# Mixture-of-experts rows that carry token, gate and residual, and a scatter of finished rows instead of gathers

## Chip, cores and metric

The kernel runs as one program on one core of a Trainium2 chip. The metric is the device time of one execution in microseconds (us), smaller is better.

## What is computed

The input is 2048 tokens (4 batches of 512) of 128 features, in fp32. Six residual steps follow each other: FFN, causal attention of two kinds, FFN, mixture of experts (MoE), linear attention, MoE. The change touches the two MoE steps and what feeds and follows them:

```python
def _L1_ffn_ref(x, Wr, W1, W2):                 # x: layernormed tokens, 8 experts, capacity 256
    probs = softmax(xf @ Wr); eidx = argmax(probs); p_tok = probs[eidx]
    rank = number of earlier tokens with the same expert
    keep = rank < cap                           # later tokens of a full expert are dropped
    xe = xf[dispatch]                           # the rows of each expert
    h = maximum(einsum('ecd,edf->ecf', xe, W1), 0)
    ye = einsum('ecf,efd->ecd', h, W2) * (p_tok * valid)
    y = zeros.at[dispatch].add(ye)              # back to the tokens; a dropped token gets 0

x = x + 0.5 * _L1_ffn_ref(_layernorm(x), ...)   # MoE 0
x = x + _L1_attn_ref(_layernorm(x), ...)
x = x + 0.5 * _L1_ffn_ref(_layernorm(x), ...)   # MoE 1, the result
```

## The kernel before

The five engines run programs of their own, written out by hand, which meet in semaphores. `s[...]` are semaphores, `hold` is a wait that also counts. B = 4 batches, NT = 4 tiles of 128 tokens in a batch, E = 8 experts with CAP = 256 rows, NG = 2 tiles of them. `x[b]` holds the residual stream of a batch on chip, one token to a partition and tile. Index n = 8m + e counts the experts of both MoE steps m.

The way of a token through MoE step m is this.

- `choose` and `place` on VectorE (DVE) pick the expert, the gate (`gate_all`, line 1034) and the slot of every token (`slot_all`, line 1040). A dropped token gets a spare slot behind the 2048 real ones.
- `scatter` on GpSimd (POOL, line 569) sends the layernormed rows (128 floats) of a batch to their slots in the DRAM array `xe_scr`, by four indirect DMAs of 128 rows each. In the first MoE step they lie between the `rsqrt` steps of the layernorms, in the second in the loop at line 698.
- `experts` on SyncE (SP, the queue of plain DMAs, line 479) loads an expert's 256 rows (`rows_in`) into one of four buffers `xg`, and stores the finished rows (`answer`) in slot order to `ye_scr`.
- TensorE (PE, line 1670) turns the rows, multiplies by the two weights; ScalarE (ACT) and DVE apply the relu, and DVE copies the product out of PSUM (line 1218). The order is the same in every expert: `up(e+1)`, `turn_rows(e+2)`, `down(e)`.
- After all eight experts, `gather` on POOL (line 577) fetches a batch's finished rows back from `ye_scr` by `slot_all`, again by four indirect DMAs, and `combine` on DVE (line 1220) multiplies by the gate and adds to `x[b]`. After MoE 1 sixteen indirect DMAs (line 720), sixteen DVE steps (line 1371) and four stores of `x[b]` to `out` (line 538) end the program.

The spare part of `xe_scr` is never read; the real part is set to zero in the first microseconds (line 344), since an expert with fewer than 256 tokens leaves slots empty. The stores at lines 339 to 347 and these share the semaphore `pad_zero`, which SP (line 424), DVE (line 1191) and `scatter` wait for.

The linear attention begins per batch with `combine`, `moments` (DVE), `rsqrt` (POOL), `normalise_entry` (DVE) and `turn_entry` (PE). Batches 0 and 1 are entered one after the other, batches 2 and 3 inside the loop over `attend`. The batch ends with `leave`, `normalise_exit`, `choose`, `place_exit` and the next `scatter`.

## Time and profile before

| | us |
|---|---|
| runs shown | 706.55, 710.32, 709.92 (median 709.92) |
| the profiled execution's own time | 705.89 |
| its span (first to last instruction) | 704.1 |
| PE busy, matmul | 506.5 (72%) |
| PE busy, weight loads | 323.5 (46%) |
| DVE busy | 365.7 (52%) |
| ACT busy | 196.7 (28%) |
| POOL busy | 181.9 (26%) |
| DMA, bytes moved | 74.16 MB, 105 GB/s on average |

The span is cut into stages by the semaphores. In us from its start: first FFN to 108, attention to 355, second FFN and placing to 415, experts of MoE 0 to 453, fetching rows and entering the linear attention to 500, the linear attention to 632, last scatter and experts of MoE 1 to 676, the end to 704. An engine's busy share over the whole span is a mean over these stages, and a change counts only where the chain of waits passes. The chain of waits lists, in order of time, the work that ended last; DMA there is a transfer that was waited for, "issue" is time in which the engine waited for nothing that the profile shows. The granted clock of PE is 1.0 or 0.5 of 2.4 GHz in a stretch, a value between them is a mean.

### The profile page before, as it was taken

The numbers are of one execution on the slowest core, as the hardware profiler recorded it, in microseconds if no ns is written. First come the engines' busy times: TensorE is split into PE (matmuls) and PEld (weight loads), VectorE is DVE, ScalarE is ACT, GpSimd is POOL, SyncE is SP. The second block draws the span as 40 slices with busy tenths as digits, with TensorE's granted clock in tenths as the row PEclk, the third lists the DMA queues.
The fourth block names the chain that finished last, engine by engine and source line by source line (L and its number), as shares of the span: only waits on it lengthen the run. The fifth ranks groups of instructions, "written<-read, shape, count | busy, mean of one in ns | idle before, by whom it ended". The sixth has DMA issues, their size and how long they took to land.

```text
span 704.1 us, 9924 instructions
## 1 busy us (share of the span) xinstructions
PE 506.5 (72%) x3706; PEld 323.5 (46%) x3706; DVE 365.7 (52%) x950; ACT 196.7 (28%) x278; POOL 181.9 (26%) x208
## 2 busy tenths in 40 slices
PE   1777775998899999988686639634788888735930
PEld 1654322445444544533475528522454655424920
DVE  4555482668667676820655412135778777330221
ACT  1454313451543245065235002112123111101200
POOL 8564360000101010010023350044402022031035
PEclk9999896999999999999999559956999999656975
DMA  7537877332633422060430021107652620001213
GB/s 267 210 117 244 266 246 197 120 99 62 139 101 89 126 80 80 29 159 15 134 106 16 19 64 49 38 27 178 186 149 54 190 70 16 1 16 52 61 41 101
DMA packets 61471, 74.16 MB, mean 105 GB/s; under 512 B 6772, under 2 KB 38128, under 8 KB 61168
## 3 DMA queue, kind: packets, MB, share of 16 engines
q1 hardware_dynamic: 59376, 69.34, 33.6%
q0 software_dynamic: 2048, 4.20, 2.1%
q8 instruction: 29, 0.48, 0.3%
q14 instruction: 18, 0.15, 0.1%
HBM read 42.97 MB, written 30.41 MB: 104 GB/s over the span
## 4 chain that ended last, share of the span: by engine, by line
PE 46%; DVE 17%; POOL 8%; SPq 8%; issue 8%; DMA 7%; ACT 5%; POOLq 0%; DVEq 0%; ACTq 0%
PE ps_accum L1379 21%; PE ps_pair L1379 15%; PE ps_turn L1379 5%; POOL xe_scr L574 3%; DMA sb_ring<-sb_qs 3%; SPq L358 2%; DVE sb_work L1133 2%; PE ps_turn L1387 2%; POOL sb_work L720 2%; POOL sb_rstd L558 2%; DVE sb_work L1271 2%; DVE sb_mpart L1059 1%; SPq L352 1%; DVE sb_stats L960 1%; DVE sb_values L969 1%
## 5 line engine op out<-in xcount | busy, mean ns | idle before, releaser
L812 ACT ACTIVATE sb_work<-ps_pair 128x1024 f32<-128x1024 f32 x80 | 80.3, 1026 | 50.7 <-PE ps_pair L1379 49.8
L1379 PE MATMUL ps_pair<-sb_ring,sb_xsets 128*128 128x512 f32 x160 | 64.6, 480 | 11.4 <-DMA sb_ring<-sb_qs 5.7
L1059 DVE TENSOR_REDUCE sb_mpart<-ps_turn 128x4 f32<-128x512 f32 x80 | 55.0, 687 | 31.2 <-PE ps_turn L1379 31.1
L1059 DVE TENSOR_REDUCE sb_mpart<-ps_accum 128x4 f32<-128x512 f32 x80 | 55.0, 688 | 19.2 <-PE ps_accum L1379 18.2
L1379 PE MATMUL ps_accum<-sb_work,sb_v_aug 128*32 128x128 f32 (+3 forms) x768 | 57.7, 394 | 0.3 <-ACT sb_work L812 0.3
L1379 PE MATMUL ps_turn<-sb_ring,sb_m_sets 128*128 128x512 f32 x80 | 39.5, 494 | 10.0 <-DVE sb_mpart L1059 9.8
L1379 PE MATMUL ps_accum<-sb_ring,sb_m_sets 128*128 128x512 f32 x80 | 41.8, 523 | 4.5 <-DVE sb_mpart L1059 3.9
L1379 PEld LDWEIGHTS ps_pair<-sb_ring,sb_xsets 128*128 128x128 f32 x160 | 30.7, 199 | 22.5 <-issue 10.7
L624 POOL TENSOR_TENSOR sb_e_pad<-sb_v_next,sb_y_ar 128x128 f32<-128x128 f32 x16 | 7.3, 457 | 127.2 <-DVE sb_y_ar L1103 127.2
L1271 DVE TENSOR_TENSOR sb_work<-ps_pair,sb_cst 128x1024 f32<-128x1024 f32 x32 | 37.5, 1214 | 2.2 <-PE ps_pair L1379 2.2
L1133 DVE TENSOR_TENSOR sb_work<-ps_pair,sb_cst 128x1024 f32<-128x1024 f32 x32 | 37.7, 1218 | 0.9
L556 POOL TENSOR_SCALAR sb_ve<-sb_mv 128x4 f32<-128x4 f32 x24 | 5.6, 233 | 124.5 <-DVE sb_mv L963 124.3
L1379 PE MATMUL ps_pair<-sb_y_tmp,sb_mw 128*128 128x256 f32 x128 | 34.1, 414 | 1.9 <-ACT sb_y_tmp L862 1.9
L574 POOL DMA_INDIRECT xe_scr<-sb_values,sb_slot_all x16 | 15.9, 994 | 73.4 <-DVE sb_slot_all L1040 69.8
L1387 PE MATMUL ps_turn<-sb_cst,sb_values 128*128 128x128 f32 x48 | 10.3, 354 | 34.1 <-DVE sb_values L969 29.6
L1379 PE MATMUL ps_accum<-sb_mw,sb_work 128*128 128x128 f32 x256 | 31.3, 276 | 2.3 <-issue 2.3
L1379 PE MATMUL ps_pair<-sb_xs,sb_w1r 128*128 128x512 f32 x64 | 22.1, 470 | 15.0 <-DVE sb_xs L979 7.4
L1379 PEld LDWEIGHTS ps_accum<-sb_mw,sb_work 128*128 128x128 f32 x256 | 30.0, 192 | 2.8 <-issue 2.6
L1218 DVE COPY sb_e_pad<-ps_accum 128x256 f32<-128x256 f32 x16 | 6.8, 425 | 44.7 <-PE ps_accum L1379 44.7
L1379 PE MATMUL ps_pair<-sb_ring,sb_ka_stk 128*128 128x512 f32 x64 | 24.4, 492 | 7.6 <-DVE sb_work L1271 4.9
L734 ACT COPY sb_xnT<-ps_turn 128x512 f32<-128x512 f32 x16 | 9.3, 583 | 70.6 <-PE ps_turn L1387 70.6
L1379 PEld LDWEIGHTS ps_pair<-sb_y_tmp,sb_mw 128*128 128x128 f32 x128 | 25.4, 210 | 6.6 <-ACT sb_y_tmp L862 3.4
(242 smaller groups left out, 1002.2 us busy)
## 6 DMA issues: line engine op xcount, KB each, us to landing
sb_m_sets<-q_scr SPq DMA_DIRECT2D x16, 256.0 KB
sb_xsets<-k_scr SPq DMA_DIRECT2D x16, 256.0 KB
sb_ka_stk<-mk_scr SPq DMA_DIRECT2D x4, 1024.0 KB
sb_mw<-in_mw SPq DMA_DIRECT2D x16, 256.0 KB, 5.6
sb_ka_stk<-mk_scr SPq DMA_DIRECT2D x8, 512.0 KB
q_scr<-sb_qs SPq DMA_DIRECT2D x12, 256.0 KB, 3.1
k_scr<-sb_ks SPq DMA_DIRECT2D x12, 256.0 KB, 3.9
sb_ring<-k_scr SPq DMA_DIRECT2D x64, 48.0 KB
```

What stands on the lines that cost most here:

```text
L358: sp.dma_start(ring[VW * hl:VW * hl + 3 * HD, i, hl].bitcast(F32), head_rows(q_scr, b, HL * hs + hl, 3 * HD)).then_inc(done, 16)
L558: pool.tensor_tensor(rstd[i][:], ve[i][:], const("minus_half"), ALU.pow).then_inc(s["rstd"], 1)
L574: pool.indirect_dma_start(xe_scr, bass.IndirectOffsetOnAxis(ap=places[:, t:t + 1], axis=0), rows_out[:, t, :], None).then_inc(s["scattered ...
L624: pool.tensor_tensor(dst, value, answer, ALU.subtract).then_inc(s["err_pad"], 1)
L720: pool.indirect_dma_start(y_last[:, b, t, :], None, ye_scr, bass.IndirectOffsetOnAxis(ap=slot_all[:, i:i + 1], axis=0)).then_inc(last_gath ...
L734: act.copy(dst, bank[:]).then_inc(s["x2_ready"], 1)
L812: act.activation(banks[:, 2 * i:2 * i + 2], pair[u % 2][:], ACT.Exp, scale=SCALE).then_inc(s["exp_done"], 1)
L1059: dve.tensor_reduce(mpart[:, m // NPAIR, m % NPAIR, :], max_banks[m % 2][:].rearrange("p (h k) -> p h k", h=HL), AX.X, ALU.max).then_inc(s ...
L1133: dve.tensor_tensor(work[:, n % 4].rearrange("p a (h q) -> p (a h) q", h=HL), pair[n % 2][:].rearrange("p a (h q) -> p (a h) q", h=HL), bc ...
L1271: dve.tensor_tensor(work[:, n % 4].rearrange("p a (h q) -> p (a h) q", h=HL), pair[n % 2][:].rearrange("p a (h q) -> p (a h) q", h=HL), bc ...
L1379: return pe.matmul(dst, lhsT, rhs, start=start, stop=stop, skip_group_check=True)
L1387: last = pe.transpose(tile(dst, t), src[:, t, :], ident)
```

## The change

Each expert row becomes RW = 258 floats wide: the layernormed row (128), the token number (`ID`), the gate (`GATE`), and the residual row (`OLD`, 128). There is an `xe_scr` and a `y_scr` for each MoE step. DVE writes residual, gate and token number straight into the row buffers (`wide_rows`, which lies over the attention's `ring`, for MoE 0; the two buffers of `exit_rows` for MoE 1). The residual is also stored by token to `y_scr` (`keep_old`), which serves dropped tokens. The copy out of PSUM becomes two DVE steps, product times gate plus residual. POOL converts an expert's token numbers to integers and scatters the finished rows to `y_scr` while the next expert computes. After MoE 0, SP loads `x[b]` from `y_scr`; after MoE 1 one DMA copies `y_scr` to `out`. The 1 MB of `xe_scr` rows and the spare half of `ye_scr` are no longer zeroed at the start. In their place six DMAs per program fill both `xe_scr` with harmless rows just ahead of the loads of the expert weights: four of 2048 pieces of 512 B, two of 2048 pieces of 8 B. `ring` is set to zero again by POOL before `scatter_back(0)`.

```diff
+RW = 2 * D + 2
+ID, GATE, OLD = D, D + 1, D + 2
+        "spill_ids": np.kron(NTOK + (NTOK // P) * p + np.arange(NTOK // P)[None, :], [[1.0, 0.0]]),
 # SP, at the start: four zeroing DMAs of 512 KB removed; pad_zero is waited for as 80, was 144
-            for half in range(2):
-                r0 = half * NTOK // 2
-                for dst in (xe_scr[r0:r0 + NTOK // 2], ye_scr[NTOK + r0:NTOK + r0 + NTOK // 2]):
-                    sp.dma_start(dst.rearrange("(p r) d -> p r d", p=P), zero[:, 0:1024]).then_inc(s["pad_zero"], 16)
 # SP, after the attention's last loads, ahead of the expert weights
+            for scr in xe_scr:
+                spill = scr[0:NTOK].rearrange("(p r) d -> p r d", p=P)
+                for c, src in ((0, bc(const("ident"), NTOK // P)), (OLD, bc(const("ident"), NTOK // P)),
+                               (ID, const("spill_ids").rearrange("p (r d) -> p r d", d=2))):
+                    sp.dma_start(spill[:, :, c:c + src.shape[2]], src).then_inc(s["spill_in"], 16)
+            def keep_old(m, b):
+                sp.dma_start(tile_rows(y_scr[m], b), rows_out[m][b][:, :, OLD:RW]).then_inc(old_kept[m][b % 2], 16)
             def experts(m):
-                sp.wait_ge(s["scattered"], 16 * NT * B * (m + 1))
+                for i in range(2):
+                    sp.wait_ge(sent[m][i], 16 * NT * B // (m + 1))
+                    hold(sp, old_kept[m][i], 16 * B // (m + 1))
+                sp.wait_ge(s["spill_in"], 96)
                 for e in range(4):
                     rows_in(m, e)
-                for e in range(E):
-                    if e + 4 < E:
-                        rows_in(m, e + 4)
-                    answer(m, e)
+                for e in range(4, E):
+                    rows_in(m, e)
+                for kept in ye_kept:
+                    hold(sp, kept, 16 * E * (m + 1))
             def rows_in(m, e):
                 if n >= 4:
                     sp.wait_ge(s["xg_t"], n - 3)
+                    sp.wait_ge(s["places_in"], n - 3)
+                    sp.wait_ge(s["ye_evac"], n - 3)
+            for b in range(B):
+                hold(sp, s["ffn_x"], B + b + 1)
+                keep_old(0, b)
             experts(0)
+            for b in range(B):
+                sp.dma_start(x[b][:], tile_rows(y_scr[0], b)).then_inc(x_loaded[b], 16)
+            hold(sp, s["zeroed"], 18)
 # SP, loop of the linear attention: keep_old(1, b - 1) after load_l1(b + 1, 1)
             experts(1)
-            for b in range(B):
-                sp.wait_ge(s["mixed"], NT * (B + b + 1))
-                sp.dma_start(tile_rows(out, b), x[b][:]).then_inc(s["out_done"], 16)
+            sp.dma_start(out.rearrange("(p r) d -> p (r d)", p=P),
+                         y_scr[1][0:NTOK].rearrange("(p r) d -> p (r d)", p=P)).then_inc(s["out_done"], 16)
 # POOL
+            def places_of(n):
+                pool.wait_ge(xg_loaded[n % 4], 16 * (n // 4 + 1))
+                if n >= 4:
+                    pool.wait_ge(ye_kept[n % 2], 16 * NG * ((n - 2) // 2))
+                pool.tensor_copy(places_back[:, n % 4, :], xg[:, n % 4, :, ID]).then_inc(s["places_in"], 1)
+            def scatter_back(m):
+                for kept in old_kept[m]:
+                    hold(pool, kept, 16 * B // (m + 1))
+                places_of(E * m)
+                for e in range(E):
+                    n = E * m + e
+                    if e + 1 < E:
+                        places_of(n + 1)
+                    pool.wait_ge(s["places_in"], n + 1)
+                    hold(pool, s["ye_evac"], n + 1)
+                    for g in range(NG):
+                        pool.indirect_dma_start(y_scr[m], bass.IndirectOffsetOnAxis(ap=places_back[:, n % 4, g:g + 1], axis=0),
+                                                ye[n % 2][:, g, :], None).then_inc(ye_kept[n % 2], 16)
 # POOL: scatter(m, b) of rows_out[m][b] into xe_scr[m]; its first call of a step also waits for spill_in 96
+            pool.memset(ring[:, 0:2].bitcast(F32), 0.0).then_inc(s["zeroed"], 1)
+            pool.memset(ring[:, 2, 0, 0:B * NT * RW - 2 * HL * T].bitcast(F32), 0.0).then_inc(s["zeroed"], 1)
+            scatter_back(0)
-            gather(0)                       # and gather(1) to gather(3) among the rsqrt, base and low_queries
...
-            for b in range(B):              # line 717: the sixteen gathers
-                for t in range(NT):
...
+            scatter_back(1)
 # DVE, place
-                dve.scalar_tensor_tensor(out=gate_all[:, NT * b:NT * (b + 1)],
+                dve.scalar_tensor_tensor(out=rows_out[r // B][b][:, :, GATE],
                                          in0=r1[6][:], scalar=0.5, in1=r1[3][:],
                                          op0=ALU.mult, op1=ALU.mult)
+                dve.tensor_scalar(rows_out[r // B][b][:, :, ID], spare[:], float(-NTOK), None, ALU.add)
 # DVE, experts
-                    dve.tensor_copy(ye[:, n % 2].rearrange("p g d -> p (g d)"), accum[n % 2][:, 0:NG * D]).then_inc(s["ye_evac"], 1)
+                    for g in range(NG):
+                        last = dve.scalar_tensor_tensor(out=ye[n % 2][:, g, :], in0=accum[n % 2][:, g * D:(g + 1) * D],
+                                                        scalar=xg[:, n % 4, g, GATE:GATE + 1], in1=xg[:, n % 4, g, OLD:RW],
+                                                        op0=ALU.mult, op1=ALU.add)
+                    last.then_inc(s["ye_evac"], 1)
 # DVE: combine(b) becomes entry(b): wait for x[b]'s load, then moments; the sixteen steps at line 1371 go
```

The order of POOL moves at two places. Around the experts of MoE 0, from the last scatter to the second `rsqrt`, it read before (`L585` is a gather, `sb_h_act` and `sb_v_low` are buffers of the linear attention):

```order
L676 MEMSET sb_v_high 128x1024
L679 MEMSET sb_h_act 128x32 x2
L679 MEMSET sb_v_low 128x32
L679 MEMSET sb_v_high 128x32
L585 DMA sb_e_pad<-ye_scr,sb_slot_all 128x128 x4
L556 TENSOR_SCALAR sb_ve_0<-sb_mv_0 128x4
L558 TENSOR_TENSOR sb_rstd_0<-sb_ve_0,sb_cst 128x4
L585 DMA sb_e_pad<-ye_scr,sb_slot_all 128x128 x4
```

and of the change (`sb_places_back` are the integer token numbers, `sb_y_tmp0` and `sb_y_tmp1` hold finished rows; line numbers are those of the changed file):

```order
L703 MEMSET sb_v_high 128x32
L706 MEMSET sb_ring 128x4096
L707 MEMSET sb_ring 128x32
L596 CAST sb_places_back<-sb_expert_rows 128x2 x2
L610 DMA y_scr0<-sb_y_tmp0,sb_places_back 4096x128 x2
L596 CAST sb_places_back<-sb_expert_rows 128x2
L610 DMA y_scr0<-sb_y_tmp1,sb_places_back 4096x128 x2
```

The pair of the last two rows repeats with the buffers in turn, to eight scatters of two DMAs, and the first `rsqrt` follows directly; no gather is left.

On SP the end of the program read before (`L494` loads an expert's rows, `L500` stores them):

```order
L494 DMA sb_e_pad<-xe_scr 128x2x128 x5
L500 DMA ye_scr<-sb_e_pad 128x2x128
L494 DMA sb_e_pad<-xe_scr 128x2x128
L500 DMA ye_scr<-sb_e_pad 128x2x128 x5
L538 DMA out<-sb_x 128x4x128 x4
```

and of the change, from the last `keep_old`:

```order
L483 DMA y_scr<-sb_exit_rows 128x4x128 x3
L504 DMA sb_expert_rows<-xe_scr 128x2x258 x8
L551 DMA out<-y_scr 16x16384
```

The eight stores of finished rows have left SP for POOL, and four stores of `x` have become one copy from DRAM to DRAM, laid out as 16 pieces of 64 KB.

## Rows read from the trace of the kernel before

**Rows 1.** Page, chain that ended last: shares of the span by engine.

```profile
PE 46%; DVE 17%; POOL 8%; SPq 8%; issue 8%; DMA 7%; ACT 5%; POOLq 0%; DVEq 0%; ACTq 0%
```

**Rows 2.** Timeline after the last experts: start us, us, engine line op, tiles, count, idle before.

```profile
675.82 0.42 DVE L1218 COPY sb_e_pad<-ps_accum 128x256 f32<-128x256 f32 x1 [2.16 <-PE ps_accum L1379]
678.83 1.00 POOL L720 DMA_INDIRECT sb_work<-ye_scr,sb_slot_all  x1 [41.15 <-DMA ye_scr<-sb_e_pad]
...
686.38 15.26 SPq L538 DMA_DIRECT2D out<-sb_x  x4
...
697.62 0.94 POOL L720 DMA_INDIRECT sb_work<-ye_scr,sb_slot_all  x1 [0.30 <-issue]
```

**Rows 3.** Windows, the stretch of the end: busy us of each engine, PE clock, DMA share, GB/s.

```profile
677.00:704.00 27.00, 0.00 (x0) 0.00 (x0) 4.56 (x16) 0.00 (x0) 15.16 (x16) 0.54 0.29 83
```

**Rows 4.** Timeline from the last expert of MoE 0 to the first batch's entry.

```profile
452.60 0.42 DVE L1218 COPY sb_e_pad<-ps_accum 128x256 f32<-128x256 f32 x1 [2.16 <-PE ps_accum L1379]
455.64 1.02 POOL L585 DMA_INDIRECT sb_e_pad<-ye_scr,sb_slot_all  x1 [37.95 <-DMA ye_scr<-sb_e_pad]
...
462.00 1.14 DVE L1224 SCALAR_TENSOR_TENSOR sb_x<-sb_e_pad,sb_gate_all,sb_x 128x128 f32<-128x128 f32 x4 [8.98 <-DMA sb_e_pad<-ye_scr,sb_slot_all]
```

**Rows 5.** Chain of waits, transfers around the experts and two later combines: start, us, what.

```profile
412.56 2.22 DMA xe_scr<-sb_v_next,sb_slot_all
414.80 2.23 DMA sb_e_pad<-xe_scr
...
478.55 1.06 DVE sb_x L1224 x4
...
526.71 1.06 DVE sb_x L1224 x4
```

**Rows 6.** Chain of waits, the first two DMAs of a scatter in the linear attention.

```profile
587.32 0.75 issue
588.07 1.09 POOL xe_scr L574
589.15 0.31 issue
589.46 0.97 POOL xe_scr L574
```

**Rows 7.** Timeline, pace of the experts of MoE 0.

```profile
427.23 0.43 DVE L1218 COPY sb_e_pad<-ps_accum 128x256 f32<-128x256 f32 x1 [4.31 <-PE ps_accum L1379]
...
430.96 0.42 DVE L1218 COPY sb_e_pad<-ps_accum 128x256 f32<-128x256 f32 x1 [2.71 <-PE ps_accum L1379]
...
432.49 0.38 PE L1677 MATMUL ps_turn<-sb_cst,sb_e_pad 128*128 128x128 f32 x2
```

**Rows 8.** Timeline of SP around the place of the fill.

```profile
316.17 0.60 SPq L400 DMA_DIRECT2D sb_ring<-sb_qs  x1
343.01 0.35 SPq L477 DMA_DIRECT2D sb_mw<-in_mw  x1
```

**Rows 9.** Chain of waits, the first scatter of MoE 0.

```profile
378.15 1.25 POOL xe_scr L574
```

**Rows 10.** Page, DMA issues: KB of each, median us from issue to landing.

```profile
q_scr<-sb_e_pad SPq DMA_DIRECT2D x1, 1024.0 KB, 7.3
...
v_scr<-sb_values SPq DMA_DIRECT2D x4, 256.0 KB, 2.7
```

**Rows 11.** Timeline, POOL's memset of the ring, and DVE at the wait for `pad_zero`.

```profile
2.97 6.92 POOL L551 MEMSET sb_ring<- 128x8192 f32 x1
...
26.78 1.12 DVE L969 TENSOR_SCALAR sb_y_ar<-sb_x,sb_mv,sb_rstd 128x128 f32<-128x128 f32 x4 [1.58 <-POOL sb_rstd L558]
28.00 0.87 DVE L960 BATCH_NORM_STATS2 sb_stats<-sb_x 128x6 f32<-128x128 f32 x4
```

**Rows 12.** Timeline, small steps of `place`.

```profile
388.59 0.16 DVE L1033 TENSOR_TENSOR sb_r<-sb_r,sb_spare 128x4 f32<-128x4 f32 x1
388.67 0.15 DVE L1034 SCALAR_TENSOR_TENSOR sb_gate_all<-sb_r,sb_r 128x4 f32<-128x4 f32 x1
```

155 lines of the change are left out of this document (67 added, 88 removed).

## The prediction

> **What bounds the kernel now.** I read the share of the chain first: PE holds 46% of it, but DVE, POOL, the queues, transfers and "issue" hold the rest [rows 1]. So much of the time is hand-over, not arithmetic, and the two MoE steps are full of it. I then read the timeline from the end backwards. The last product leaves PSUM at 675.82 + 0.42 = 676.24. From there to the end of the span at 704.1 pass 27.9 us in which PE does nothing; POOL is busy for 15.2 us of the last 27.0 [rows 2, 3]. It issues sixteen gathers one after the other, from 678.83 to 697.62 + 0.94 = 698.56, that is 1.25 us for each; DVE's steps and the four stores of SP hang on them. The bound of the end is POOL's issue of indirect DMAs.
>
> Then I read the same place after MoE 0. The product is ready at 453.02, the first gather starts at 455.64, and the first batch's combine runs from 462.00 to 463.14 [rows 4]. Each later combine costs the chain another 1.06 us: three such pieces stand in it, the first at 478.55, the last at 526.71 [rows 5]. Between these places, the experts run at a pace that PE sets: two copies out of PSUM follow each other after 430.96 - 427.23 = 3.73 us [rows 7]. In the linear attention POOL's scatters stand on the chain too, 0.75 us of issue and then 1.09, 0.31, 0.97 us for the first two DMAs [rows 6].
>
> **The change part by part.**
>
> *The end.* Sixteen gathers, sixteen DVE steps and four stores go. In their place stands only what cannot lie beside the experts: the last expert's two scatters and the copy. The copy out of PSUM becomes two DVE steps of 128 columns. The gather's combine has four such steps in 1.14 us [rows 4], 0.29 each, so the pair costs 0.57 where 0.42 stood, +0.15: ready at 676.39. POOL then needs 0.75 of issue, 1.09 for the first DMA and 0.31 to the second [rows 6]: 678.54. A scatter lands 2.22 us after its start [rows 5]: 680.76. The copy of 1 MB I cannot read anywhere. A store of 256 KB lands in 2.7 us, one of 1024 KB in 7.3, with other stores in the queue [rows 10]. The lower bound is 2.7. The upper is 14.6, twice 7.3, if the bytes read from DRAM and the bytes written to it add. I take 6.5, near the row of equal size but with an empty queue. The end is then 687.3 instead of 704.1: **-16.8 us**, with -20.6 and -8.7 as ends. For the copy the Trainium skill, page "DMA: Bandwidth & Descriptors", section "Anatomy of one DMA — SWDGE (gpsimd) path", gives a fixed 2.0 us plus bytes at 436 GB/s; my estimate by that is 4.4 us, and the sum would be 2.1 us lower. The page's fit is of another issuing engine, and no run here shows a copy from DRAM to DRAM.
>
> *Entering the linear attention.* The same steps after 453.02: +0.15, 0.75 + 1.09 + 0.31, 2.22 to land, which is 457.54. SP then loads `x[0]`, 256 KB; a load of 128 KB takes 2.23 [rows 5], a store of 256 KB 2.7 [rows 10]; I take 3.0, so 460.5, against 463.14 before: **-2.6 us**, between -3.4 and -1.4 for loads of 2.2 to 4.2. What is late next is the same as before, `moments` on DVE.
>
> *Later combines.* Their three pieces vanish, and `moments` waits for loads that came in about 460: **-3.2 us** (3 x 1.06). DVE is in program order here and the pieces are on the chain, so I count all; the lower bound is 0, if PE or a load ends the wait in their place. The gathers among POOL's small steps go too; no wait of the chain ends on them, so 0.
>
> *The experts.* Rows grow from 512 to 1032 B. The first load of a step is on the path: 2.23 for 128 KB [rows 5]; with twice the bytes I take 2.9, and 0.1 more for the last scatter before it: +0.8 twice, **+1.6 us**, ends 0 and +4.4 (double both). In the steady state loads have slack: the load of expert 4 now waits for the first product, 427.23 + 0.6, and lands 2.9 later at 430.7, before PE wants it at 432.49 [rows 7]. POOL's work beside the experts is 0.75 + 1.09 + 0.31 + 0.97 = 3.1 us for an expert and about 0.2 for the conversion, under the 3.73 of the pace; hidden, with 0.4 to spare. The eight stores that leave SP were hidden before and save nothing.
>
> *`place`.* One step of 128x4 more, eight times. Two such steps start 388.67 - 388.59 = 0.08 us apart where none waits for the other [rows 12]; +0.08 x 8 = **+0.6 us**, from 0 to 1.3 (0.16 each).
>
> *The 32 scatters to the experts.* POOL makes as many rows as before, and 0.97 us a DMA [rows 6] was the same for 128 rows wherever I looked. I take **0**. The trace has no indirect DMA with wider rows; the upper bound is time in proportion to bytes, below.
>
> *Start.* Four zeroing DMAs go. DVE's wait for `pad_zero` ends at 28.00, and its own work before ended at 27.90 [rows 11]: 0.1 us at most, counted 0. Removing 2 MB of traffic hardly helps, since DVE and PE are not waiting for it.
>
> *The fill.* Six DMAs, 4 MB in pieces of 512 B and 4096 pieces of 8 B, go into SP's queue between 316.8 and 343.0, where SP issues nothing [rows 8]. They must be done when POOL starts the first scatter at 378.15 [rows 9]. Four times 7.3 [rows 10] is 29 us; the small pieces, priced as the 512 B ones, another 15. From about 320 that ends at 364: hidden, **0**. The expert weights behind them have until 414.80. The memset of `ring` takes about 3.5 us, half of 6.92 [rows 11], on POOL between 417 and 427, when it has nothing else; `keep_old` on SP has no one behind it who waits. Both 0.
>
> Sum: -16.8 - 2.6 - 3.2 + 1.6 + 0.6 = **-20.4 us**. Against the profiled execution's own time, 705.89, this is 685.5; the span would be 683.7. The median of the runs shown is 4 us higher, 709.92, and the four times fall into two pairs about 706 and 710. I put the forecast on their mean, 708.2: **687.8 us**.
>
> **The rivals.**
>
> *Wider rows cost POOL in proportion (slower).* If an indirect DMA with rows of 1032 B takes twice 0.97 us, each scatter adds 0.97. Of the 32, the chain passes 24: eight in MoE 0, sixteen in the linear attention, where the `rsqrt` of the next batch is queued behind them. That is +23.3 us: 711. It outweighs the gain from 0.85 us more per DMA. For it: nothing in the trace excludes it. Against: the gap between DMAs and the 0.97 look like a cost of rows, not of bytes, since gathers and scatters take the same (0.94 and 0.97). Chance 5%.
>
> *The fill is late.* If it starts only at 343 and takes 44 us, it ends at 387 and the first scatter, with `rsqrt` and the second FFN behind it, waits 9 us: 697. Should the small pieces cost several times a 512 B piece, it is more. A rule speaks for this one: the Trainium skill, page "DMA: Bandwidth & Descriptors", section "Specifications", has writes under 512 B done as read-modify-write. No small strided stores are priced in this trace. Chance 10%.
>
> *POOL does not keep the pace.* If the conversion, its wait on its own result and the two DMAs take 4.2 us instead of 3.3, POOL falls behind by 0.5 us an expert and 3.5 us by the eighth, in both steps, and DVE's reuse of `ye` waits in the end: +7, 695. For it: only 0.4 us to spare. Against: the 0.75 of issue shrinks when POOL is never idle. Chance 14%.
>
> *The copy at the end is slow.* At 14.6 us: +8.1, 696. Only 16 pieces of 64 KB, one for each DMA engine, read and written in the same memory. Chance 11%.
>
> The forecast as it stands has 60%, between 683 and 692. Slower than before needs the first rival, or two others at their worst: 6% with "over 0.5%", the least that a measurement of this kernel can tell from no change (3.5 us); within 0.5% 2%; faster 92%. The range runs from 681, where the short copy, the short loads and the lower pair of times meet, to 699, which takes in the three mild rivals.
>
> **What would show it.** In the profile after: 64 indirect DMAs on POOL, all about 0.97 us, with the `rsqrt` of each later batch directly behind; if those into `xe_scr` are longer, the first rival. PE's pace in the experts stays at 3.73, and the last scatter starts 0.75 us after the last DVE step; a larger lag is the third. From that step to the end of the span 11 us. No `L1224` pieces in the chain. The first scatter of MoE 0 still at 378, released by DVE and not by a DMA. I am wrong if the span stays above 697.

## The result, and the profile after

The changed kernel takes **685.94 us** (median of four runs, 684.23 to 691.97) beside 708.23 for the kernel before in the same comparison: a ratio of 0.970, 95% interval 0.963 to 0.977. Five more rounds gave 686.97 against 709.29, ratio 0.968 (0.963 to 0.972). The forecast was 687.8 in a range of 681 to 699, faster with 92%.

The profiled execution took 686.1 us with a span of 684.3. Its page: the chain that ended last, the costliest groups and two lines of the DMA issues (KB each, us to landing).

```profile
PE 49%; DVE 17%; POOL 8%; issue 8%; ACT 6%; DMA 5%; SPq 5%; POOLq 0%; DVEq 0%; ACTq 0%
...
L610 POOL DMA_INDIRECT y_scr<-sb_y_tmp,sb_places_back x32 | 30.8, 961 | 40.9 <-issue 33.0
...
L588 POOL DMA_INDIRECT xe_scr<-sb_exit_rows,sb_slot_all x16 | 15.9, 995 | 73.8 <-DVE sb_slot_all L1061 70.1
...
sb_expert_rows<-xe_scr SPq DMA_DIRECT2D x16, 258.0 KB, 2.8
...
xe_scr<-sb_cst SPq DMA_DIRECT2D x4, 1024.0 KB, 13.6
```

PE's share of the chain rose from 46 to 49% [rows 1]; SP's queue and the transfers lost 5 points together. An indirect DMA costs POOL 0.96 to 1.0 us, with rows of 512 B (L610) as with rows of 1032 B (L588).

The timeline of the end (start us, us, engine line op), which answers to [rows 2]:

```profile
673.31 0.61 DVE L1241 SCALAR_TENSOR_TENSOR sb_y_tmp<-ps_accum,sb_expert_rows 128x128 f32<-128x128 f32 x2 [2.16 <-PE ps_accum L1397]
674.70 0.96 POOL L610 DMA_INDIRECT y_scr<-sb_y_tmp,sb_places_back  x1 [1.14 <-issue]
675.96 0.96 POOL L610 DMA_INDIRECT y_scr<-sb_y_tmp,sb_places_back  x1 [0.30 <-issue]
678.29 0.59 SPq L551 DMA_DIRECT2D out<-y_scr  x1
```

Two scatters and one copy stand where sixteen gathers stood. The first of them starts 0.78 us after DVE's last step (673.92). The copy is issued at 678.29, lands 5.6 us later, and the span ends at 684.3, 6.0 us after the issue.

The chain of waits at the entry of the linear attention (start, us, what), which answers to [rows 4]:

```profile
457.86 2.23 DMA y_scr<-sb_y_tmp,sb_places_back
...
460.18 2.88 DMA sb_x<-y_scr
...
463.15 0.89 DVE sb_stats L977 x4
```

The last scatter's landing and the load of `x[0]` follow each other, and the moments start at 463.15.

To compare whole executions I cut each span at the same events. Below, "entry" is the row "to first moments", "linear attention" the row after it, and "end" the last row; "product" is DVE's copy or multiply that takes an expert's result out of PSUM. Both kernels were profiled twice (the second profiles are from the runs below):

| stretch, us | before | before again | after | after again |
|---|---|---|---|---|
| start to first scatter of MoE 0 | 378.15 | 378.14 | 380.77 | 380.08 |
| to its last scatter's start | 34.41 | 32.84 | 33.49 | 33.85 |
| to first product of MoE 0 on DVE | 14.67 | 15.03 | 15.40 | 16.29 |
| to last product of MoE 0 | 25.37 | 25.37 | 25.55 | 25.55 |
| to first moments | 10.57 | 10.66 | 7.94 | 7.92 |
| to last scatter's start of MoE 1 | 173.55 | 170.34 | 168.39 | 171.74 |
| to first product of MoE 1 | 13.73 | 13.90 | 16.22 | 15.95 |
| to last product of MoE 1 | 25.37 | 25.37 | 25.55 | 25.56 |
| to the end of the span | 28.28 | 28.25 | 10.99 | 10.96 |

The short stretches repeat within 0.1 us, or within 1; the long ones move by up to 3.4 us between two profiles of one program. So the end (-17.3) and the entry (-2.7) are read from one pair of profiles; the linear attention is not.

### The profile page after: what moved, and what is told of

It is laid out like the page before. It is cut to its first block, busy times and chain, and to the rows that moved or that the text cites. A ratio compares the mean times of both kernels' runs of the same rounds, so it can differ in the third digit from the quotient of the medians.

```text
span 684.3 us, 9986 instructions
## 1 busy us (share of the span) xinstructions
PE 507.8 (74%) x3706; PEld 325.3 (48%) x3706; DVE 358.5 (52%) x942; ACT 196.9 (29%) x278; POOL 188.3 (28%) x226
## 4 chain that ended last, share of the span: by engine, by line
PE 49%; DVE 17%; POOL 8%; issue 8%; ACT 6%; DMA 5%; SPq 5%; POOLq 0%; DVEq 0%; ACTq 0%
PE ps_accum L1397 22%; PE ps_pair L1397 17%; PE ps_turn L1397 5%; POOL xe_scr L588 3%; DMA sb_ring<-sb_qs 3%; SPq L355 2%; POOL sb_rstd L569 2%; DVE sb_work L1154 2%; PE ps_turn L1405 2%; DVE sb_mpart L1080 1%; DVE sb_work L1292 1%; SPq L349 1%; DVE sb_stats L977 1%; PE ps_turn L1827 1%; SPq L363 1%
## 5 line engine op out<-in xcount | busy, mean ns | idle before, releaser
L610 POOL DMA_INDIRECT y_scr<-sb_y_tmp,sb_places_back x32 | 30.8, 961 | 40.9 <-issue 33.0
L588 POOL DMA_INDIRECT xe_scr<-sb_exit_rows,sb_slot_all x16 | 15.9, 995 | 73.8 <-DVE sb_slot_all L1061 70.1
L1241 DVE SCALAR_TENSOR_TENSOR sb_y_tmp<-ps_accum,sb_expert_rows 128x128 f32<-128x128 f32 x32 | 9.7, 346 | 42.6 <-PE ps_accum L1397 42.6
L1397 PE MATMUL ps_pair<-sb_xs,sb_w1r 128*128 128x512 f32 x64 | 21.5, 460 | 13.5 <-DVE sb_xs L996 5.9
```

The costliest lines, as they stand in the source:

```text
L588: pool.indirect_dma_start(xe_scr[m], bass.IndirectOffsetOnAxis(ap=slot_all[:, i:i + 1], axis=0), rows_out[m][b][:, t, :], None).then_inc(s ...
L610: pool.indirect_dma_start(y_scr[m], bass.IndirectOffsetOnAxis(ap=places_back[:, n % 4, g:g + 1], axis=0), ye[n % 2][:, g, :], None).then_i ...
L1241: last = dve.scalar_tensor_tensor(out=ye[n % 2][:, g, :], in0=accum[n % 2][:, g * D:(g + 1) * D], scalar=xg[:, n % 4, g, GATE:GATE + 1], i ...
L1397: return pe.matmul(dst, lhsT, rhs, start=start, stop=stop, skip_group_check=True)
```

## The experiments

Every kernel is the changed one with one edit (two, where the heading names two), but for the kernel before itself. Ratios are to the kernel before. The edits are shown in part, with `...` where lines are left out.

### The changed kernel again

> The changed kernel itself, once more, to see how far two profiled runs of one program differ. Between the start and the last mask of attention the profiled run of after was 3.94 us longer than that of before (347.54 against 343.60), with no changed instruction on the way. Theory 1, run-to-run variation: the last mask of this run lies anywhere between 343 and 348 us and its distance to 347.54 is over 1 us. Theory 2, the change causes it (the zero rows that no longer travel at the start, the fill of the spill rows that SP issues from 334 us): 347.5 us again, within 0.5. Every later stretch of the table should come back within 0.5 us by either: last product to the end 11.0 us, of it the copy to the output 6.0, last product of the first experts to the first moments of the linear attention 7.9, time 684 to 688 us and 2.5 to 3.5% under before.

Measured: 686.97 us; start to first scatter 380.08, end 10.96, entry 7.92, linear attention 171.74. The end and the entry came back within 0.05 us. The last mask of attention started at 345.5, 2.0 us earlier than in the first profile of after (347.5), so half of the 3.94 us in front of it was variation. The linear attention was 3.35 us longer than in the first profile. The windows of both, 520 to 580 us (busy us by engine, then PE's granted clock, DMA share, GB/s), show what differs:

```profile
520.00:580.00 60.00, 50.96 (x538) 33.98 (x536) 44.35 (x124) 12.09 (x22) 10.35 (x12) 0.94 0.44 120
```

```profile
520.00:580.00 60.00, 53.26 (x516) 35.28 (x512) 42.39 (x120) 11.50 (x21) 10.40 (x12) 0.85 0.44 121
```

The first is after, the second the repeat: a clock of 0.94 of full speed against 0.85, and PE busy for 2.3 us more with fewer matmuls done. Over all profiles of the changed kernel and of those below that put nothing into this stretch, it took 167.8 to 168.5 us at 0.94 to 0.97 (seven profiles) and 171.7 and 172.1 at 0.85 and 0.81.

### The second mixture's scatters after the last expert

```diff
+                if m:
+                    continue
                 pool.wait_ge(s["places_in"], n + 1)
...
+                for e in range(E if m else 0):
+                    n = E * m + e
+                    for g in range(NG):
+                        pool.indirect_dma_start(y_scr[m], bass.IndirectOffsetOnAxis(ap=places_back[:, n % E, g:g + 1], axis=0),
+                                                ye[n][:, g, :], None).then_inc(ye_kept[n % 2], 16)
```

The eight experts' rows lie in `x[0]` to `x[3]`, which nobody needs any more.

> The second mixture's finished rows are kept in eight places and its 16 scatters go out after the last expert, the rest is as in the changed kernel. Theory (the gain at the end is that the way back runs beside the experts): 14 scatters at 0.96 + 0.30 us come behind the last product, so the end is 17.6 us later, some 704 us, nearly the whole gain of the change gone, with TensorE's pace in the experts unchanged. Rival A (the gain at the end is mainly that two hops through DRAM became one, whenever the scatters go): under +10 us. Rival B (the scatters beside the experts take something from them, so that moving them behind gives some back): experts faster by over 2 us, and the sum under +15.

Measured: 705.93 us, ratio 0.995 (0.992 to 0.998). Last product to the end 29.06 us where 10.99 stood, +18.1; the experts' pace is unchanged (25.55 from first to last product). The timeline, and POOL's own drain at the end by line (start after the forms):

```profile
674.63 0.98 POOL L620 DMA_INDIRECT y_scr<-sb_x,sb_places_back  x1 [12.22 <-DVE sb_x L1251]
...
693.58 0.96 POOL L620 DMA_INDIRECT y_scr<-sb_x,sb_places_back  x1 [0.30 <-issue]
```

```profile
L116 POOLq DRAIN  x1: 18672/18672/18672, 681.2 to 681.2; - x1
```

Sixteen DMAs at 1.26 us, as in [rows 2]. Theory holds, both rivals fall: all of the gain at the end is that fourteen of POOL's DMAs run beside PE. With the sixteen behind the last product, the new way back is worth nothing there (29.06 against 28.28 before).

### Straight to the output

```diff
-        y_scr = [dram(f"y_scr{m}", [2 * NTOK, D]) for m in range(2)]
+        y_scr = [dram("y_scr0", [2 * NTOK, D]), out]
...
-                                                ye[n % 2][:, g, :], None)
+                                                ye[n % 2][:, g, :], None, bounds_check=NTOK - 1, oob_is_err=False)
...
-            sp.dma_start(out.rearrange("(p r) d -> p (r d)", p=P),
-                         y_scr[1][0:NTOK].rearrange("(p r) d -> p (r d)", p=P)).then_inc(s["out_done"], 16)
-            sp.wait_ge(s["out_done"], 16)
```

> The second mixture's finished rows are scattered straight to the output, with a bound of 2,048 rows above which a row is skipped (the rows of empty slots); the plain copy of 1 MB at the end is gone. Theory (the copy is all on the path): its 6.0 us and its issue of 0.6 go, 6 to 7 us under the changed kernel, some 679.5 us. Rival A (the bound makes the scatter dearer on POOL): up to 0.3 us for each of the two last scatters and no effect on the other 14, so 5.5 us under; only at over 2.9 us a pair more would it reach the experts' 3.73 us pace (2.5 us of POOL per expert now). Rival B (writes to the output land no sooner than the copy, or the skip stalls the queue): within 2 us of the changed kernel.

Measured: 685.88 us, ratio 0.966 (0.962 to 0.970): not to be told from the changed kernel's 686.97. Last product to the end is 9.24 us instead of 10.96 to 10.99: **1.7 us, not 6**. The expectation missed what else must end. The last scatter, and POOL's drain in this kernel:

```profile
681.00 0.97 POOL L607 DMA_INDIRECT out<-sb_y_tmp,sb_places_back  x1 [0.30 <-issue]
```

```profile
L116 POOLq DRAIN  x1: 7243/7243/7243, 680.0 to 680.0; - x1
```

The drain runs from 680.0 to 687.2, 5.3 us beyond the last scatter's end at 681.97, and the span ends at 687.5. In the changed kernel:

```profile
L116 POOLq DRAIN  x1: 7300/7300/7300, 674.9 to 674.9; - x1
```

It ends at 682.2, again 5.3 us behind the last scatter (676.92), and only the copy's end lies later, by 1.8 us. With the scatters last it was 681.2 + 18.7 = 699.9, again 5.3 behind 694.5. So the copy hid 4 of its 6 us beside a drain that nobody had counted. The bound itself cost POOL 0.01 us for a DMA.

The drain is there before the change as well, and there it is what ended last:

```profile
L114 POOLq DRAIN  x1: 18492/18492/18492, 685.4 to 685.4; - x1
L114 SPq COMPARE_BRANCH  x1: 38/38/38, 703.6 to 703.6; - x1
```

It ended at 703.9, 5.3 us behind the last gather's end (698.56), and SP was done with the stores at 703.6. Shorter stores alone would have gained nothing. The 5.3 us are the same in all twelve profiles of kernels with 64 indirect DMAs (32 scatters to the experts, 32 back); in the two with 80, further below, the drain ended 6.6 us behind the last one:

```profile
L116 POOLq DRAIN  x1: 8305/8305/8305, 684.8 to 684.8; - x1
```

That is 684.8 + 8.3 = 693.1, and the last indirect DMA of that kernel (the gathers back) ended at 686.44. 5.31 / 64 and 6.62 / 80 are both 0.083 us; that the drain's tail grows with the number of indirect DMAs in the program is my estimate from these two counts.

### Direct, and each half by itself

```diff
-                    hold(pool, s["ye_evac"], n + 1)
+                    hold(pool, s["ye_half"], n + 1)
                     for g in range(NG):
+                        if g:
+                            hold(pool, s["ye_evac"], n + 1)
...
```

> Straight to the output as in a2, and each expert's first scatter waits for the first of the two products on DVE only, not for both (a semaphore of its own). What the first call showed: after the last scatter POOL's queue drains 5.3 us before the program can end, so the direct writes were worth 1.75 us at the end (9.24 against 10.97 to 11.0 us from the last product) and not 6. Theory: another 0.3 us at the end of each mixture (the two products stand 0.3 us apart), so last product to the end 8.9 to 9.0 us, last product of the first mixture to the first moments 7.6; in all 2.3 us under the changed kernel, 683.5 to 686 by the median. Rival (POOL's wait takes its 1.1 us whenever the product comes): 9.24 and 7.94 again, 1.7 us under.

Measured: 686.69 us by the median (681.55 to 693.93), ratio 0.966 (0.960 to 0.973). The end took 9.0 us as expected, the entry 7.76 (expected 7.6, so half of the gain there). The two stretches are together 2.2 us shorter than in the changed kernel; the medians do not separate such a difference, so I call this version 2 us better in these stretches and unproven in the whole.

### The zeroing back at the start

```diff
+            for half in range(2):
+                r0 = NTOK + half * NTOK // 2
+                for dst in (y_scr[0][r0:r0 + NTOK // 2], y_scr[1][r0:r0 + NTOK // 2]):
+                    sp.dma_start(dst.rearrange("(p r) d -> p r d", p=P), zero[:, 0:1024]).then_inc(s["pad_zero"], 16)
...
```

> The four DMAs of 512 KB of zeros at the start are put back (into rows of y_scr that nobody reads), with the waits on them as before the change. Theory (they cost nothing, as the prediction had it): within 1 us of the changed kernel. Rival A (they slow the first loads and scratch writes): 1 to 4 us slower, seen before 110 us. Rival B (their absence is what made the stretch to the last mask 3.94 us longer, by an order of the DMAs that came out worse): 2 to 4 us faster, last mask near 343.6.

Measured: 687.28 us, ratio 0.969 (0.965 to 0.973). No difference; the first scatter started at 383.5, later than in the changed kernel, so the missing zeroing did not delay it.

### The kernel before, once more

> The kernel before once more, for a second profile of it. Theory (run-to-run variation of the stretches): start to the last mask 343.6 us in the first profile lies outside or at the edge of what this one shows, 344 to 347 here as in the changed kernel and its variants (344.4 to 349); first scatter at 379 to 382. Rival (the change really made that stretch 2 to 4 us longer): 343.6 and 378.2 within 0.5 us again. The stretch from the first moments to the last scatter of the second mixture, 173.55 us in the first profile against 168.39 after the change: theory 172 to 173 here.

Measured, one execution: 701.73 us, span 699.9. The first scatter came at 378.14, the rival's number. The last mask came at 344.98, 1.4 us later than in the first profile (343.60), as theory had it. The linear attention came at 170.34, 3.2 us under the first profile, which is less than theory had. So neither account holds whole. The last mask's place goes along with the granted clock. The windows from 0 to 345 us of this run and of the changed kernel's repeat (the clock is the third number from the right):

```profile
0.00:345.00 345.00, 281.93 (x1884) 154.23 (x1888) 203.17 (x424) 129.75 (x157) 86.81 (x100) 0.96 0.47 135
```

```profile
0.00:345.00 345.00, 280.73 (x1868) 152.73 (x1869) 202.40 (x423) 129.75 (x157) 86.92 (x100) 0.96 0.49 135
```

| clock, 0 to 345 us | last mask, us | first scatter, us |
|---|---|---|
| 0.97, before | 343.6 | 378.15 |
| 0.96, before again | 345.0 | 378.14 |
| 0.96, changed kernel and variants, three profiles | 344.7 to 345.5 | 378.4 to 380.1 |
| 0.93 to 0.95, the same, eight profiles | 345.3 to 349.6 | 378.5 to 384.5 |

(The kernel with the fill at its start is left out, and so is the first scatter of the one with the fill twice; both are below.) At the same clock the last mask stands at the same place within 0.6 us, so up to there the change itself costs nothing that these profiles show; to the first scatter it is 0.3 to 1.9 us. Whether the change makes the lower clock there more frequent stays open: there are two profiles of the kernel before.

### The fill of the spill rows at the start

```diff
+            sp.wait_ge(s["first_loaded"], 16 * FIRST_LOADS)
+            for scr in xe_scr:
+                spill = scr[0:NTOK].rearrange("(p r) d -> p r d", p=P)
...
             sp.wait_ge(s["zeroed"], 2)
...
-            for scr in xe_scr:
-                spill = scr[0:NTOK].rearrange("(p r) d -> p r d", p=P)
...
             hold(sp, s["ma_mm"], 2 * NT * B)
```

> The fill of the spill rows (its six DMAs for both exchange buffers) goes out at the start, behind the first loads, and no longer in front of the experts' weights. Theory (the fill is hidden where it stands, though it began at 334 and not at 320 us): within 1.5 us of the changed kernel in the whole, first scatter of the first mixture at 378 to 382 us, weights issued again from about 343 us. Rival A (SP's 20 us of issuing at 334 us, or its traffic, is what made the stretch to the first scatter 2.6 us longer than before the change): 2 to 3 us faster. Rival B (at the start it delays the first loads and scratch writes that the front end waits for): 3 us or more slower, seen before 110 us.

Measured: **711.25 us**, ratio 1.005 (1.001 to 1.008): the whole gain is gone. The last mask starts at 370.5 instead of 344.7 to 349.6. SP's timeline and DVE's waits up to 110 us (waited for, us in total, times, longest):

```profile
13.68 28.14 SPq L348 DMA_DIRECT2D xe_scr<-sb_cst  x6
41.86 5.43 SPq L350 DMA_DIRECT2D k_scr<-sb_v_next  x1
```

```profile
DVE sb_stats L978 <- DMA k_scr<-sb_v_next: 23.7, 1, 23.7
```

SP needs 28 us to issue the fill, the last padding DMA stands behind it, and DVE waits 23.7 us for that one. Rival B holds. The fill is dear; it costs nothing only where it stands.

### The fill twice at its place

```diff
-            for scr in xe_scr:
+            for scr in xe_scr + more:
...
```

> The fill of the spill rows goes out twice at its place (the second time into two tables that nobody reads; the first scatter and the loads wait for all twelve DMAs). In the changed kernel SP issues it from 334.5 to 354.5 us and the weights from there to 371.6; the first scatter starts at 380.8 by its own data, the weights are wanted at 417. Theory: issuing takes 20 us more, to 374.5, the second half lands by about 390, the weights land by 397. The first scatter waits 5 to 10 us, but the last scatter is what the experts wait for, and POOL has room between the batches: 0 to 6 us slower in all. Rival A (nothing: all is covered): within 1 us. Rival B (SP's queue and the DMA engines carry the delay on to the chain, as with the fill at the start, which cost 25 us there): over 12 us slower.

Measured: 702.04 us, ratio 0.987 (0.980 to 0.994); the span 701.6, 17.3 us over after. SP's row of the second fill and POOL's first scatter in this kernel:

```profile
356.95 30.93 SPq L477 DMA_DIRECT2D more<-sb_cst  x6
```

```profile
398.46 1.24 POOL L589 DMA_INDIRECT xe_scr<-sb_wide_rows,sb_slot_all  x1 [22.74 <-DMA more<-sb_cst]
```

In after the same two places read:

```profile
334.47 20.02 SPq L476 DMA_DIRECT2D xe_scr<-sb_cst  x6
354.60 5.14 SPq L479 DMA_DIRECT2D sb_mw<-in_mw  x1
```

```profile
380.77 1.24 POOL L588 DMA_INDIRECT xe_scr<-sb_wide_rows,sb_slot_all  x1 [6.96 <-DVE sb_slot_all L1061]
```

Rival B again: the first scatter waits 17.7 us longer, and all of it arrives at the end. My expectation gave POOL room between the batches, and forgot that the `rsqrt` of the next batch is queued behind the waiting scatter, which the forecast had noted for its first rival. In after the release comes from DVE. The fill's last DMA there is issued at 349.5 (the first row: ns of an issue, least, median and most, then first and last start) and lands 14.6 us later (the second row: the issues from 349.3 on):

```profile
L476 SPq DMA_DIRECT2D xe_scr<-sb_cst x6: 606/3884/4989, 334.5 to 349.5; - x6
```

```profile
xe_scr<-sb_cst SPq DMA_DIRECT2D x1, 16.0 KB, 14.6
```

That is 364.1, 16.7 us before the first scatter starts: its whole cover. Doubled, the last landing is at 397.6, 33.5 us later; 16.7 of them are covered, and the rest is, within a microsecond, the 17.7 us that the scatter lost.

### The combines back

```diff
                 dve.wait_ge(x_loaded[b], 32)
+                for t in range(NT):
+                    dve.scalar_tensor_tensor(out=spare_rows[b % 2][:, t], in0=x[b][:, t], scalar=mv[0][:, t, 0:1], in1=x[b][:, t],
+                                             op0=ALU.mult, op1=ALU.add)
                 moments(norm_of_entry(b), x[b], b % 2)
```

> The four products of a combine (scalar_tensor_tensor on DVE, 128x128 each) are put back ahead of the moments of every batch that enters the linear attention, on dead data and with no wait. Prediction's terms: 1.06 us for each of batches 1 to 3 on the path (3.2) and one more for batch 0, so 4.2 us slower in all than the changed kernel, of it 3.2 behind the first moments. Rival A (those combines stood in slack of DVE, and the 5.2 us that the stretch from the first moments to the last scatter lost came from POOL's missing gathers): under 1.5 us slower. Rival B (all 5.2 us hung on the combines): 5 us or more slower behind the first moments.

Measured: 690.36 us, ratio 0.975 (0.967 to 0.984). The entry took 8.95 (+1.0), the linear attention 170.73 at a clock of 0.94, against 167.8 to 168.5 at such a clock: +2.2 to +2.9, for three combines. Close to the prediction's 1.06 each, a little under; both rivals fall. This is read from the stretches of one profile; the time as a whole (its interval takes in the changed kernel's 0.968) does not separate the two kernels.

### The gathers back, alone and with the combines

```diff
+            gather(0)
             rsqrt(norm_of_entry(0), 0)
+            gather(1)
             base(0)
...
```

The gathers read `y_scr[0]` into a buffer of their own. The two later ones stand where they stood before, and the unused half of `y_scr[0]` is set to zero at the start.

> The 16 gathers of the kernel before (128 rows of 512 B each, from DRAM into a dead buffer) are put back on POOL at their old places in the linear attention; nobody waits for their data. Theory (POOL has room there, the combines' 3.2 us are the term that counts and the rest is how two profiled runs differ): the first batch's gather and the second's delay rsqrt of batch 0 and 1 by POOL's time of four, up to 5 us once, since the entry's rsqrt stands behind gather 0 and gather 1 on POOL, and nothing from the later two. Since x of batch 0 lands 7.4 us after the last product now, gather 0 (5.0 us behind its wait) ends about when the moments do: +0 to 1 us; gather 1 lies behind the first rsqrt, as before: +0 to 2. Rival A (POOL's gathers took 2 us of the stretch behind the first moments, beside the combines): 2 to 4 us slower there. Rival B (nothing of the kind): under 0.5 us in all.

Measured: 691.13 us, ratio 0.973 (0.965 to 0.981). The entry took 8.03 us, but the linear attention 174.75. POOL's timeline has the gather in front of the first `rsqrt`:

```profile
467.90 0.94 POOL L731 DMA_INDIRECT sb_spare_rows<-y_scr,sb_places_back  x1 [0.30 <-issue]
468.88 0.26 POOL L574 TENSOR_SCALAR sb_ve<-sb_mv 128x4 f32<-128x4 f32 x1
```

That `rsqrt` starts 2.4 us behind the first moments (466.45) instead of 2.0.

With four products per batch on DVE that wait for the gathered rows:

> Gathers and combines both back in the changed kernel: 16 gathers of 512 B rows at their old places on POOL, and ahead of every batch's moments four products on DVE that wait for them (x plus zero times the gathered row, so the result stays). The load of x from y_scr stays. This is the whole entry as before the change, plus the 2.9 us load. Theory: last product to the first moments 13.5 us against 7.94 (gathers' 5.0 and landing 2.2 behind the last scatter's landing, 1.06 of products, less what of it the load of x covers), first moments to the last scatter of the second mixture 171 to 173 at a granted clock of 0.94 to 0.97 between 520 and 580 us, against 168 (the combines alone: 170.7; the gathers alone, at a clock of 0.91: 174.75). In all 8 to 10 us slower than the changed kernel. Rival (gathers and combines hinder each other, or each hides the other): that second stretch 169 or less, or 175 or more.

Measured: 696.65 us, ratio 0.981 (0.975 to 0.986), 9.7 us over the 686.97 of the changed kernel. The entry:

```profile
465.74 1.14 DVE L1274 SCALAR_TENSOR_TENSOR sb_x<-sb_spare_rows,sb_cst,sb_x 128x128 f32<-128x128 f32 x4 [11.46 <-DMA sb_spare_rows<-y_scr,sb_places_back]
466.91 0.87 DVE L1000 BATCH_NORM_STATS2 sb_stats<-sb_x 128x6 f32<-128x128 f32 x4
```

13.25 us from the last product to the moments (expected 13.5), and 173.80 in the linear attention, at a clock of 0.91: between the theory's 171 to 173 and the rival's 175. Cut at the moments of batches 1 and 2, the linear attention reads (us):

| | first moments to those of batch 1 | to those of batch 2 | to the last scatter's start |
|---|---|---|---|
| before, two profiles | 16.46, 16.25 | 19.31, 18.94 | 137.78, 135.15 |
| changed, nine profiles | 15.04 to 15.45 | 17.91 to 17.94 | 134.83 to 138.81 |
| combines back | 15.75 | 18.98 | 136.00 |
| gathers back | 16.07 | 19.33 | 139.35 |
| both back | 16.24 | 18.98 | 138.57 |

(The nine are the changed kernel twice and all variants but these three.) The first two columns repeat well. Their sum is 33.0 to 33.4 for the changed kernel and 35.8 and 35.2 before. Against the middle, 33.2, the combines alone add 1.5 us, the gathers alone 2.2, both together 2.0. So the gathers, which I had put at 0, are worth as much there as the combines (their 2.2 us is the size of rival A), and the two hide each other: taking out one of them alone would have gained little. The last three rows are one profile each.

In the third column the gathers' 139.35 is no price of theirs. The same part of it in that kernel and in after, from the fifth to the ninth indirect DMA of the scatters, with no gather in either:

```profile
589.26:621.68 32.42, 25.19 (x195) 16.26 (x195) 15.92 (x55) 3.15 (x6) 5.26 (x6) 0.64 0.07 25
```

```profile
582.95:612.03 29.08, 21.85 (x195) 14.07 (x195) 15.90 (x55) 3.16 (x6) 5.26 (x6) 0.79 0.08 28
```

The same 195 matmuls took 3.3 us more at a granted clock of 0.64 instead of 0.79; the twelve other profiles have 29.1 us there. So the 5.3 to 7.0 us that the two kernels with gathers stand over the level of 168 can't be put down to the gathers.

### Narrow scatters in the second mixture

```diff
-                    pool.indirect_dma_start(xe_scr[m], bass.IndirectOffsetOnAxis(ap=slot_all[:, i:i + 1], axis=0),
-                                            rows_out[m][b][:, t, :], None).then_inc(sent[m][b % 2], 16)
+                    pool.indirect_dma_start((xe_scr[0], narrow)[m], bass.IndirectOffsetOnAxis(ap=slot_all[:, i:i + 1], axis=0),
+                                            rows_out[m][b][:, t, 0:(RW, D)[m]], None).then_inc(sent[m][b % 2], 16)
...
```

> The second mixture's 16 scatters write 128 rows of 512 B each into a table of their own, instead of 1,032 B; the loads stay wide (the second mixture then computes on the filled rows alone, so its result is left out). In the changed kernel the last scatter's start lies 3.17 us before the load's issue and 6.1 us before the first turn, against 2.26 and 4.36 before the change. Theory (the wide row lands later): last scatter to the load's issue 2.2 to 2.3 us again, to the first product's copy 15.0 to 15.3 instead of 15.9 to 16.2, POOL's time per scatter 0.96 us all the same. Rival (the load waits for something else: the old rows' copy, the fill's semaphore): 3.2 us again.

Measured (688.28 us, ratio 0.973, too wide for this question): the last scatter and the load of the first expert, in this kernel and in after:

```profile
628.46 0.96 POOL L589 DMA_INDIRECT narrow<-sb_exit_rows,sb_slot_all  x1 [0.31 <-issue]
630.92 1.90 SPq L505 DMA_DIRECT2D sb_expert_rows<-xe_scr  x4
```

```profile
631.54 0.96 POOL L588 DMA_INDIRECT xe_scr<-sb_exit_rows,sb_slot_all  x1 [0.30 <-issue]
634.71 1.90 SPq L504 DMA_DIRECT2D sb_expert_rows<-xe_scr  x4
```

2.46 us from start to issue with 512 B rows, 3.17 with 1032 B (2.9 to 3.3 in all profiles with wide rows). POOL's 0.96 is the same, so the width costs 0.7 us of landing and nothing of issue. To the first product 15.70 instead of 15.9 to 16.2, less of a gain than expected. The way to the first product of MoE 1 in three pieces says where the rest went (us; "turn" is PE's first instruction on the rows):

| | last scatter to load's issue | to the turn | to the first product |
|---|---|---|---|
| before, two profiles | 2.25, 2.25 | 2.10, 2.18 | 9.38, 9.47 |
| after | 3.17 | 2.91 | 10.14 |
| narrow scatters | 2.46 | 2.77 | 10.47 |

The third piece begins at a granted clock of 0.5. The window from the turn to the step of the granted clock to 1.0, in before, after and the narrow scatters:

```profile
641.07:645.28 4.21, 3.70 (x9) 2.76 (x10) 0.00 (x0) 0.37 (x1) 0.00 (x0) 0.50 0.35 100
```

```profile
637.62:643.91 6.29, 5.23 (x13) 3.61 (x14) 0.69 (x1) 1.13 (x3) 0.37 (x2) 0.50 0.26 86
```

```profile
633.69:640.65 6.96, 5.90 (x14) 4.10 (x15) 0.69 (x1) 1.24 (x3) 0.37 (x2) 0.50 0.27 84
```

The clock rose to 1.0 at 4.2 us before the change, at 6.3 after it and at 7.0 here. Of the 0.7 us that the narrow rows gain, 0.3 goes back through this.

## Why the prediction was right, by its own steps

*The end*: -16.8 forecast, **-17.3** measured (28.28 to 10.99, both repeated within 0.05). The copy took 6.0 us from its issue to the end of the span where 6.5 was taken; the bounds of 2.7 and 14.6 were far off on both sides. The Trainium skill's fit (page "DMA: Bandwidth & Descriptors", section "Anatomy of one DMA — SWDGE (gpsimd) path"), 4.4 us by my estimate, was 1.2 us short of the copy's landing (5.6 us after its issue). What the step did not see is POOL's drain. Before the change it ended last, 0.3 us behind the stores; after the change the copy did, 1.8 us behind it. That the stores ended so close to the drain is why the step came out right without it. At a copy of 4.4 us the end would have come near the drain's floor, at 2.7 it would have been no more than 0.3 us lower still.

*Entering the linear attention*: -2.6 against **-2.6** (and -2.7 in the repeats); the load of `x[0]` took 2.88, 3.0 was taken.

*Later combines*: -3.2. Put back alone they cost 2.7 (or 2.2 to 2.9). But the same step said that the gathers among POOL's small steps cost 0, and that part is wrong: up to the moments of batch 2, where two of the three combines lie, the gathers alone cost 2.2 us, the combines alone 1.5 and both 2.0. There the change gained 1.8 to 2.8 us (33.0 to 33.4 against 35.2 and 35.8), by taking out both. Behind that, two profiles of one kernel differ by up to 3.5 us with the clock, and the third combine can't be read from before and after. So the size is about right and its cause half right.

*The experts*: +1.6 forecast; **+3.6** measured (means of two profiles each: +1.0 and +2.3 in front of the first products, and 0.18 in each run of products, since a pair of DVE steps stands where a copy stood). This is the term that was mis-sized. In MoE 1 the load goes out 0.9 us later behind the last scatter (3.17 against 638.98 - 636.72 = 2.26 before) where 0.1 was allowed, the load itself takes 2.9 as forecast, and PE's first products take another 0.7, with the clock at half speed for 6.3 us instead of 4.2; the forecast had no term for that. PE's pace stays at 3.73. POOL needs 3.2 us for an expert (0.78 from DVE's step to the first DMA, 0.96 + 0.30 + 0.96 for the two, 0.20 for the conversion), where 3.3 was forecast, and the last scatter starts 0.78 us behind DVE's last step: the third rival falls.

*The 32 wide scatters*: 0, right; the first rival falls at 0.96 us a DMA. *Start*: 0, right by the zeroing put back. *`place`*: +0.6, too small to see.

*The fill*: 0 in the time, and the forecast's 364 us for its end was met (364.1), by luck: two errors cancelled. It began at 334.5 and not at 320, since SP's waits on PE's scores of the last batch stand in front of it, though nothing is issued between them. And it took 29.6 us from the first issue to the last landing, not 44. The six landings in after, as the semaphore that they share counts them, are at 342.1, 347.9, 350.9, 356.0, 361.8 and 364.1; the third and the sixth are the small pieces, 3.0 and 2.2 us behind the large DMA before them, where the large ones take 5.1 to 5.9. So 2048 pieces of 8 B cost about half of 2048 pieces of 512 B, priced alike in the forecast, and not several times as much, as the second rival feared. That rival would have needed a landing 17 us later; the experiment with the fill doubled has just its mechanism, and its 697 with a larger delay: 702. The rule that speaks for it, read-modify-write of pieces under 512 B (the Trainium skill, "DMA: Bandwidth & Descriptors", "Specifications"), made no price here above that of the large pieces; what the same bytes would cost without it, no run shows.

*Sum*: -20.4 forecast, -19.8 between the two first spans, -22.3 between the medians. The steps as read one by one (-17.3, -2.6, about -2 to -3, +3.6) give -18 to -19. The first spans come closer to the forecast in part by luck: in that pair the first scatter came 2.6 us later and the linear attention was 5.2 us shorter, and both differences carry the clock. No rival came: POOL keeps the pace, the copy is not slow.

## What to carry to other kernels

Work that serialises on POOL behind the last product is cheap when each piece goes out as soon as its expert is done: fourteen indirect DMAs at 1.26 us were worth the whole gain at the end. When a final transfer is removed, look first at what else has to end, here POOL's drain 5.3 us behind its last indirect DMA. Two pieces of work that hide each other, here gathers and combines, have to go together before the time moves by their price. Before a stretch is compared between two profiles, compare its granted clock. A bulk fill that costs nothing has a place and a margin: doubled it cost 15 to 17 us, put at the start 23 to 25, each time through the instruction queued behind the one that waited.

## What the runs showed of the hardware

- POOL's drain at the end of the program ended 5.3 us after its last indirect DMA in twelve profiles with 64 indirect DMAs (703.9 us before the change; 682.2, 687.2 and 699.9 in three of the others) and 6.6 us after it in the two with 80, though such a DMA's data lands 2.2 us after its start.
- SP took 20 to 23 us to issue six DMAs of small strided pieces in the middle of the program, 28 us at the start and 31 us when repeated at once; most of its other DMAs take 0.3 to 1 us each, but the one right behind the fill took 5.1 to 6.2.
- In the fill of after, 2048 pieces of 512 B landed 5.1 to 5.9 us behind the DMA before them, 2048 pieces of 8 B 3.0 and 2.2 us.
- An indirect DMA of 128 rows cost POOL 0.96 us at 512 and at 1032 B a row, 0.97 to 0.98 with a bound; wide rows landed 0.7 us later.
- Two profiles of one program differed by 3.2 and 3.4 us in the linear attention. For the changed kernel the longer one had a granted clock of 0.85 instead of 0.94 of full speed between 520 and 580 us; for the kernel before it was 0.94 against 0.97.
- A part of 195 matmuls took 32.4 us at a granted clock of 0.64 and 29.1 at 0.79, with the same work on every engine.
